# The last batches' output pairs of an attention and mixture-of-experts kernel, put in another order

## The chip, the cores and the metric

One NeuronCore of a Trainium2 chip runs the whole program. The metric is the device time of one execution in microseconds (us), lower is better.

## The reference

A transformer layer in float32, for an input x of 8 batches x 1024 tokens x 256 features:

```python
x = x + layernorm(attention(layernorm(x)))      # 16 heads of 16, causal mask
x = x + layernorm(ffn(layernorm(x)))

def ffn(hidden):                                # 8 experts, the best two of each token count
    scores = softmax(flat @ router_weight.T + router_bias)
    topk_w, topk_idx = top_k(scores, 2)
    gate, up = split(flat @ gate_up_proj[e] + gate_up_bias[e])
    act = (clip(up, -7, 7) + 1) * min(gate, 7) * sigmoid(1.702 * min(gate, 7))
    down = act @ down_proj[e] + down_bias[e]
    return sum over the two experts of topk_w * down
```

## The kernel before

The program has three stages with a barrier of all engines between them. **The attention stage** computes attention, the first residual sum, the router and the place of every token's row in a buffer `xs`, sorted by expert. **The expert stage** works through 136 tiles of 128 rows of `xs`, one expert each, and adds the results into `acc`. **The combine stage** normalises and adds the second residual. The change is in the attention stage only.

The attention stage is one list of **slots**, which every engine walks through in the same order; each engine's queue is in program order, and semaphores tie the queues together. There are 32 quads (four heads of one batch), and a quad takes `NE` = 12 slots: in slot g, TensorE makes four blocks of exponents' scores (line 853), ScalarE their exponentials (700), GpSimd masks the diagonal blocks (403, eight slots of twelve), TensorE weighs the values (872). Quad 31 ends with slot 383. Eighteen slots ahead runs the pass for the row maxima (TensorE 834, VectorE 485 and 488, in a ring of three PSUM banks), which ends at slot 365. A head of this pass takes three slots; in the trace, heads begin at 1194.6 us (slot 336), 1202.5 (339), 1227.9 (348) and 1237.0 (351). Attention's output goes to HBM twice a quad: the first half is stored at c = 6 of the quad (335), the second at c = 2 of the next (338), and with it the softmax denominators. c is the slot's number within its quad. At c = 0 SP also issues the twelve head loads of the quad after next (268, 270).

**Pairs.** The output side works on 32 pairs of token tiles (256 tokens), four to a batch; pair r has the start slot `C_AT[r]`. Relative to it:
- SP loads denominators and outputs at -8 (351, 355). VectorE inverts the denominators at -6 (580), SP stores them (317) and reloads them spread over partitions at -5 (324), with the pair's x behind (327), for which it first waits for the sum of pair r - 2 (`c_x1`).
- GpSimd multiplies outputs by inverses at -3 (431).
- TensorE projects at 0 and +1 (944), ScalarE copies at +1 (784), VectorE takes moments at +3 and +4 (600, 650), GpSimd turns them into a scale and a shift at +5 (438 to 444), ScalarE normalises at +6 (789), GpSimd adds x at +7 (452).
- The second norm runs likewise at +9, +10 and +11 (607, 650, 438 to 444, 798); SP stores the sum at +9 (358).
- TensorE transposes at +14 (965) and makes the router's logits at +15 and +16 (976); VectorE picks the best at +16 to +18 (655, 613, 619).

For the pairs before `LATE` = 28 the start slots are 12 apart: pairs 24 to 27 (batch 6) have 339, 351, 363 and 375. The last batch has 388, 391, 396 and 399.

**Groups.** The rows of a group of pairs are ranked together: `choose` on VectorE (520 to 533), `rank` on TensorE (988, 991), `place` on VectorE (545 to 567), which ends in the slot numbers `slot_i`. GpSimd then scatters the rows to `xs`, one indirect DMA of 128 rows for each tile and choice (462): 16 for a batch, 8 for half a batch. Batches 0 to 6 are a group each, the last batch is two. `G_AT` is the start of a group's last pair. A whole batch's scatters start 30 slots after it and are spread by `EVEN` over 36 slots; a half batch's start 22 after it, one a slot.

```python
    C_AT = [NE * (r + 4) + 3 for r in range(LATE)] + [NE * QUADS + d for d in (4, 7, 12, 15)]
    GROUPS = [range(PER * b, PER * b + PER) for b in range(B - 1)] + [range(LATE, LATE + 2), range(LATE + 2, PAIRS)]
    S_AT = [G_AT[n] + (EVEN[k] if n in STEADY else 22 + k) for n, k in SCATTERS]
```

Slots from 384 on have no attention work left: there only the pairs' own waits set the time, and each queue runs on in the order above. At the very end SP waits until all scatters have landed and writes one block of zeros behind each expert's rows (372 to 375, eight DMAs, each with an address read from SBUF first), and VectorE computes the table of tiles (659 to 685). SP waits for the zeros, and the barrier follows.

## Time and profile before

| what | us |
|---|---|
| median of three runs | 2316.2 (2313.4 to 2321.1) |
| the profiled execution | 2312.5 |
| its span, first to last instruction | 2310.7 |
| attention stage up to the last copy of its output | 1322.0 |
| from there to the expert stage's first load | 103.6 |
| from that load to the end of the span | 885.1 |

Busy time over the span, from the page of the profile: TensorE 2003.9 us (87%), VectorE 1687.1 (73%), ScalarE 1132.6 (49%), GpSimd 975.5 (42%). Such a share is a mean over stages with different limits, so it is to be read stage by stage. PE is TensorE's matmuls, PEld its weight loads, DVE VectorE, ACT ScalarE, POOL GpSimd, SP the queue that issues most DMAs (SPq). An arrow in a wait names what ended it.

### The profile page before, as it was taken

How to read it: one execution, taken by the hardware profiler on the slowest of the kernel's cores; microseconds unless marked ns; L12 is line 12 of the kernel's file. 1: busy time of each engine (PE TensorE's matmuls, PEld its weight loads, DVE VectorE, ACT ScalarE, POOL GpSimd, SP SyncE). 2: the span in 40 equal slices, each digit the busy share in tenths (PEclk: the TensorE clock that was granted, in tenths of full speed). 3: DMA queues.
4: the chain of work that ended last, by engine and by line, in shares of the span. 5: the costliest groups of instructions: out<-in, count | busy, mean ns of one | idle time of the engine just before them, and what ended most of it. 6: DMA issues, size and time to landing. Idle time of an engine off the chain costs nothing. (4 is left out here: it accounts for less than half of the span.)

```text
span 2310.7 us, 51852 instructions
## 1 busy us (share of the span) xinstructions
PE 2003.9 (87%) x13629; PEld 1307.3 (57%) x13630; DVE 1687.1 (73%) x5978; ACT 1132.6 (49%) x2647; POOL 975.5 (42%) x1583
## 2 busy tenths in 40 slices
PE   5499999999999999999989842999999999999960
PEld 4243444444444444444333331998898888888950
DVE  2487768787888888888868232777777777777768
ACT  3156667777777777777766720222222222222220
POOL 4122334445646465555544553333333333333326
PEclk9789999999999999999999955999999999999985
DMA  5926575767666666768584223887787778778766
GB/s 156 183 63 145 125 167 150 183 153 178 146 167 140 163 145 168 152 154 172 111 215 95 97 82 136 238 242 233 238 239 236 236 233 235 232 238 238 236 193 237
DMA packets 259627, 412.94 MB, mean 179 GB/s; under 512 B 37136, under 2 KB 194960, under 8 KB 253200
## 3 DMA queue, kind: packets, MB, share of 16 engines
q1 hardware_dynamic: 220432, 367.20, 58.6%
q0 software_dynamic: 29824, 35.54, 7.4%
q10 hardware_dynamic: 9216, 8.39, 1.1%
q8 instruction: 66, 1.08, 0.2%
q14 instruction: 89, 0.73, 0.1%
HBM read 288.30 MB, written 122.14 MB: 178 GB/s over the span
## 5 line engine op out<-in xcount | busy, mean ns | idle before, releaser
L700 ACT ACTIVATE pw<-ps_e 128x512 f32<-128x512 f32 (+3 forms) x1536 | 688.7, 493 | 310.2 <-PE ps_e L853 301.7
L1244 PE MATMUL ps_g<-x_t,w_gu 128*128 128x128 f32 x4384 | 541.7, 277 | 28.1 <-ACT x_t L1175 21.9
L834 PE MATMUL ps_s<-ks,qs 96*128 96x512 bf16 (+3 forms) x1536 | 492.9, 336 | 67.0 <-DVE mrow L499 34.1
L1244 PEld LDWEIGHTS ps_g<-x_t,w_gu 128*128 128x128 f32 x4384 | 515.2, 192 | 59.2 <-issue 49.1
L485 DVE CUSTOM_DVE_ANT_0 summed<-ps_s,c 128x128 bf16<-128x128 f32 (+3 forms) x1024 | 480.3, 482 | 83.2 <-PE ps_s L834 79.4
L853 PE MATMUL ps_e<-qs,ks 98*128 98x512 bf16 (+3 forms) x1536 | 487.1, 331 | 3.2 <-ACT pw L700 3.0
L488 DVE TENSOR_REDUCE cmax<-ps_s 128x1 f32<-128x512 f32 x512 | 351.5, 686 | 142.7 <-PE ps_s L834 139.9
L834 PEld LDWEIGHTS ps_s<-ks,qs 96*128 96x128 bf16 x1536 | 152.8, 101 | 405.0 <-issue 120.2
L872 PE MATMUL ps_o<-pw,vs 128*32 128x512 f32 (+3 forms) x3072 | 332.7, 506 | 4.9 <-ACT ot L714 2.8
L1196 ACT ACTIVATE d_y<-biased,weight 128x256 f32<-128x256 f32 x136 | 69.1, 508 | 490.3 <-DVE biased L1155 490.3
L403 POOL TENSOR_SCALAR_AFFINE_SELECT pw<-pw 128x512 f32<-128x512 f32 x256 | 162.1, 633 | 310.9 <-ACT pw L700 310.8
L1210 POOL DMA_INDIRECT acc<-d_y,place_now x136 | 214.8, 1580 | 120.5 <-issue 74.5
L1273 PE MATMUL ps_y<-space,act_h 128*128 x1088 | 258.1, 380 | 0.8 <-DVE act_h L1148 0.8
L1136 DVE TENSOR_SCALAR gate<-ps_g,space 128x128 f32<-128x128 f32 x548 | 154.4, 345 | 105.4 <-issue 94.1
L853 PEld LDWEIGHTS ps_e<-qs,ks 98*128 98x128 bf16 x1536 | 149.8, 98 | 110.2 <-ACT pw L700 19.9
L1273 PEld LDWEIGHTS ps_y<-space,act_h 128*128 128x128 f32 x1088 | 196.1, 190 | 22.6 <-issue 1.5
L1203 POOL TENSOR_TENSOR place_now<-place,c 128x1 int32<-128x1 int32 x136 | 24.9, 183 | 430.9 <-ACT d_y L1196 430.5
L1141 DVE TENSOR_SCALAR up<-ps_g,space 128x128 f32<-128x128 f32 x548 | 154.3, 344 | 9.0 <-PE ps_g L1244 0.2
L462 POOL DMA_INDIRECT xs<-c_h,slot_i x128 | 131.5, 1027 | 33.2 <-issue 32.6
L872 PEld LDWEIGHTS ps_o<-pw,vs 128*32 128x32 f32 x3072 | 60.9, 108 | 121.9 <-issue 80.1
L414 POOL DMA_DIRECT2D qs<-mrow x128 | 81.5, 637 | 109.6 <-DVE mrow L499 105.3
L1179 ACT ACTIVATE sig<-gate 128x512 f32<-128x512 f32 x137 | 86.3, 630 | 79.2 <-DVE gate L1136 79.2
(136 smaller groups left out, 2289.6 us busy)
## 6 DMA issues: line engine op xcount, KB each, us to landing
w_gu<-in_gate_up SPq DMA_DIRECT2D x138, 1024.0 KB, 5.0
qk_parts<-space SPq DMA_DIRECT2D x128, 192.0 KB, 7.2
qs<-qk_parts SPq DMA_DIRECT2D x192, 128.0 KB, 7.3
ks<-qk_parts SPq DMA_DIRECT2D x192, 128.0 KB, 7.8
d_xin<-xs SPq DMA_DIRECT2D x139, 130.5 KB, 2.5
v_aug<-space SPq DMA_DIRECT2D x32, 512.0 KB, 7.4
vs<-v_aug SPq DMA_DIRECT2D x32, 512.0 KB, 11.6
o_t<-ot SPq DMA_DIRECT2D x64, 256.0 KB, 2.8
```

The costliest lines, as they stand in the source:

```text
L403: pool.affine_select(diagonal, diagonal, [[0, 4], [1, P]], ALU.is_ge, 0.0, base=0, channel_multiplier=-1).then_inc(cut_done, 1)
L485: dve.tensor_tensor_reduce(summed[:, m % RJ, 0:w], ps_s[:, m % RS, 0:w], after[:, HALF - w:HALF], 1.0, LOWEST, ALU.add, ALU.max, dst).then ...
L488: dve.reduce_max(dst, ps_s[:, m % RS, 0:w], AX.X).then_inc(s_cmax, 1)
L700: act.activation(pw[:, n % RP, 0:w], ps_e[:, n % RE, 0:w], ACT.Exp, scale=SCALE).then_inc(e_done, 1)
L834: pe.matmul(ps_s[:, m % RS, 0:w], qs[0:ROWS, slot, i * P:(i + 1) * P], ks[0:ROWS, slot, k0:k0 + w], start=True, stop=True).then_inc(s_scor ...
L853: pe.matmul(ps_e[:, n % RE, 0:w], ks[0:ROWS_M, slot, j * P:(j + 1) * P], qs[0:ROWS_M, slot, q0:q0 + w], start=True, stop=True).then_inc(e_ ...
L872: last = pe.matmul(ps_o[s * QUAD:(s + 1) * QUAD, at:at + w], vs[:, u, j, s], pw[:, (g * 4 + s) % RP, 0:w], start=(j == 0), stop=(c + 1 in ...
L1136: last = dve.tensor_scalar(gate[:, u, m], ps_g[:, u, 0, m], b_gu[:, bass.ds(e, 1), m], LIMIT, ALU.add, ALU.min)
L1141: last = dve.tensor_scalar(up[:, m], ps_g[:, u, 1, m], b_gu[:, bass.ds(e, 1), KI + m], LIMIT + 1, ALU.add, ALU.min)
L1210: pool.indirect_dma_start(out=acc, out_offset=bass.IndirectOffsetOnAxis(place_now[:, u:u + 1], 0), in_=y[:, u], in_offset=None, compute_op ...
L1244: last = pe.matmul(ps_g[:, u, half, m % KI], w_gu[:, u, k, m * P:(m + 1) * P], x_t[:, u, k], start=(k == 0), stop=(k == KT - 1))
L1273: last = pe.matmul(ps_y[:, u, 0:D], act_h[:, u, m], w_dn[:, bass.ds(e, 1), m], start=(m == 0), stop=(m == KI - 1))
```

## The change

1. **Batch 6 every six slots.** `C_AT` of pairs 24 to 27 becomes 339, 345, 351 and 357.
2. **Halves.** Batch 6 is ranked in two groups of two pairs as well. The half groups get later steps relative to their start (`choose` 19 to 21, `rank` 23, `place` 23 to 26, scatters from 27 on). The scatters of batch 5 now follow one a slot from slot 357 on, those of batch 6 in slots 372 to 379 and 384 to 391, those of batch 7 in 415 to 422 and 433 to 440.
3. **The last pairs side by side.** `C_AT` of pairs 28 to 31 becomes 387, 388, 405 and 406. Loads and reciprocals of 30 and 31 stay as early as before by larger negative offsets (-17, -15, -12), while their projections come later in TensorE's order.
4. **VectorE multiplies and adds.** For pairs 24 to 31 the multiply by the inverses (offset -2 or -4) and the sum with x (+7) are VectorE's instead of GpSimd's. The reload of the inverses goes to offset -4 (pairs 24 to 29).
5. **Zero blocks on two queues.** Experts 0 to 3 by SP, 4 to 7 by ScalarE's queue, both after the same waits.

```diff
@@ -100,13 +100,16 @@
     A_AT = [BEGIN - 18 + 3 * a for a in range(EARLY)] + [BEGIN - 5, BEGIN + 2] + [NE * (a - 6) - 4 for a in range(6, PAIRS)]
     FIRST_EVEN = 6
     LATE = PAIRS - PER
-    C_AT = [NE * (r + 4) + 3 for r in range(LATE)] + [NE * QUADS + d for d in (4, 7, 12, 15)]
-    GROUPS = [range(PER * b, PER * b + PER) for b in range(B - 1)] + [range(LATE, LATE + 2), range(LATE + 2, PAIRS)]
+    C_AT = [NE * (r + 4) + 3 for r in range(LATE)] + [NE * QUADS + d for d in (3, 4, 21, 22)]
+    QUICK = LATE - PER
+    for r in range(QUICK, LATE):
+        C_AT[r] = C_AT[QUICK] + 6 * (r - QUICK)
+    GROUPS = [range(PER * b, PER * b + PER) for b in range(B - 2)] + [range(r, r + 2) for r in range(QUICK, PAIRS, 2)]
     G_AT = [C_AT[pairs[-1]] for pairs in GROUPS]
     SCATTERS = [(n, k) for n, pairs in enumerate(GROUPS) for k in range(len(pairs) * 2 * TOPK)]
-    STEADY = range(B - 1)
+    STEADY = range(B - 2)
     EVEN = [30 + d for turn in range(0, 4 * NE, NE) for d in (turn, turn + 6, turn + 7, turn + 9, turn + 10)]
-    S_AT = [G_AT[n] + (EVEN[k] if n in STEADY else 22 + k) for n, k in SCATTERS]
+    S_AT = [G_AT[n] + (30 + k if n == B - 3 else EVEN[k] if n in STEADY else 27 + k) for n, k in SCATTERS]
     SLOTS = range(A_AT[0] - 6, max(S_AT) + 2)
     MOMENTS = [(r, k) for slot, k, r in sorted((C_AT[r] + 3 + 6 * k, k, r) for r in range(PAIRS) for k in range(2))]
 
@@ -114,10 +117,15 @@
 
         return [n for n, start in enumerate(G_AT) if start + (steady if n in STEADY else late) == slot]
 
+    def rows_due(steady, quick, late, slot):
+
+        return [r for r, start in enumerate(C_AT) if start + (steady if r < QUICK else quick if r < LATE + 2 else late) == slot]
+
     def pairs_due(early, steady, slot):
 
         return [n for n, start in enumerate(A_AT) if start + (early if n < FIRST_EVEN else steady) == slot]
     LOADS = 12
+    NEVER = SLOTS.stop + NE * QUADS
     Q_STORES = 4
 
     base, table, expert_f = kept
@@ -255,6 +263,15 @@
 
             return sum(2 * PER * TOPK for e in range(b % 2, b, 2))
 
+        def clear_ends(engine, experts):
+
+            engine.wait_ge(zero_at_ready, 1)
+            for u in range(2):
+                engine.wait_ge(scattered[u], (T // P) * TOPK // 2 * 16)
+            for e in experts:
+                row = engine.value_load(zero_at[0:1, e:e + 1], min_val=0, max_val=E * REGION - P)
+                engine.dma_start(xs[bass.ds(row, P), :], blank[:, 0:ROW]).then_inc(zeros_out, 16)
+
         block = ctx.enter_context(nc.Block())
 
         @block.sync
@@ -311,11 +328,11 @@
                         load_heads(early)
                     for early in range(SETS):
                         load_values(early)
-                for r in due(C_AT, -6, g):
+                for r in rows_due(-6, -6, -15, g):
                     u, b, j = r % 2, r // PER, r % PER
                     sp.wait_ge(c_den, r + 1)
                     sp.dma_start(rden[r].rearrange("h (c t) -> (h c) t", c=P // H), den[:, u]).then_inc(rd_out[u], 16)
-                for r in due(C_AT, -5, g):
+                for r in rows_due(-5, -4, -12, g):
                     u = r % 2
                     sp.wait_ge(rd_out[u], (r // 2 + 1) * 16)
                     if r >= 2:
@@ -343,7 +360,7 @@
                 if 2 <= quad < 10 and c == 10:
                     sp.dma_start(acc_v[:, (quad - 2) * 2:(quad - 1) * 2],
                                  blank[:, 0:1024].unsqueeze(1).broadcast_to([P, 2, 1024])).then_inc(acc_zero, 16)
-                for r in due(C_AT, -8, g):
+                for r in rows_due(-8, -8, -17, g):
                     u, b, j = r % 2, r // PER, r % PER
                     sp.wait_ge(o_out[j // 2], (4 * b + 4) * 16)
                     if r >= 2:
@@ -367,12 +384,7 @@
                     sp.dma_start(b_dn.rearrange("p e d -> p (e d)"),
                                  down_bias.rearrange("(a e) d -> a (e d)", a=1).broadcast_to([P, E * D])).then_inc(biases_in, 16)
 
-            sp.wait_ge(zero_at_ready, 1)
-            for u in range(2):
-                sp.wait_ge(scattered[u], (T // P) * TOPK // 2 * 16)
-            for e in range(E):
-                row = sp.value_load(zero_at[0:1, e:e + 1], min_val=0, max_val=E * REGION - P)
-                sp.dma_start(xs[bass.ds(row, P), :], blank[:, 0:ROW]).then_inc(zeros_out, 16)
+            clear_ends(sp, range(0, E // 2))
             for u in range(2):
                 sp.wait_ge(x1_out[u], PAIRS // 2 * 16)
                 sp.wait_ge(o_out[u], QUADS * 16)
@@ -424,13 +436,13 @@
                     pool.wait_ge(a_negated, a + 1)
                     pool.wait_ge(a_rooted, a + 1)
                     pool.tensor_tensor(a_shift[:, u], a_minus[:, u], a_rstd[:, u], ALU.mult).then_inc(a_shifted, 1)
-                for r in due(C_AT, -3, g):
+                for r in due(C_AT[0:QUICK], -3, g):
                     u = r % 2
                     pool.wait_ge(o_loads[u], (r // 2 + 1) * KT * 16)
                     pool.wait_ge(rd_loads[u], (r // 2 + 1) * KT * 16)
                     pool.tensor_tensor(o_in[:, u], o_in[:, u], rd_in[:, u], ALU.mult).then_inc(c_on, 1)
-                for k, offset in enumerate((5, 10)):
-                    for r in due(C_AT, offset, g):
+                for k, offsets in enumerate(((5, 4, 4), (10, 10, 10))):
+                    for r in rows_due(*offsets, g):
                         u, n = r % 2, MOMENTS.index((r, k))
                         pool.wait_ge(c_agg, n + 1)
                         if r >= 2:
@@ -442,7 +454,7 @@
                         pool.wait_ge(c_negated, n + 1)
                         pool.wait_ge(c_rooted, n + 1)
                         pool.tensor_tensor(c_shift[:, k, u], c_minus[:, k, u], c_rstd[:, k, u], ALU.mult).then_inc(c_shifted, 1)
-                for r in due(C_AT, 7, g):
+                for r in due(C_AT[0:QUICK], 7, g):
                     u = r % 2
                     pool.wait_ge(c_yn, r + 1)
                     pool.wait_ge(cx_in[u], (r // 2 + 1) * 16)
@@ -574,16 +586,30 @@
                     if 0 <= m < HEADS * NM:
                         maximum(m)
                     if s == 0:
-                        for r in due(C_AT, -6, g):
+                        for r in rows_due(-6, -6, -15, g):
                             u = r % 2
                             dve.wait_ge(den_in[u], (r // 2 + 1) * 16)
                             dve.reciprocal(den[:, u], den[:, u]).then_inc(c_den, 1)
+                        for r in rows_due(NEVER, -2, -4, g):
+                            u = r % 2
+                            dve.wait_ge(o_loads[u], (r // 2 + 1) * KT * 16)
+                            dve.wait_ge(rd_loads[u], (r // 2 + 1) * KT * 16)
+                            dve.wait_ge(c_on, r)
+                            dve.tensor_tensor(o_in[:, u], o_in[:, u], rd_in[:, u], ALU.mult).then_inc(c_on, 1)
+                        for r in rows_due(NEVER, 7, 7, g):
+                            u = r % 2
+                            dve.wait_ge(c_yn, r + 1)
+                            dve.wait_ge(cx_in[u], (r // 2 + 1) * 16)
+                            dve.wait_ge(x1_out[u], r // 2 * 16)
+                            dve.wait_ge(c_hn, r - 1)
+                            dve.wait_ge(c_x1, r)
+                            dve.tensor_tensor(x1_sb[:, u], y[:, u], cx[:, u], ALU.add).then_inc(c_x1, 1)
                         for n in groups_due(19, 19, g):
                             choose(n, 0)
                     if s == 1:
-                        for n in groups_due(22, 19, g):
+                        for n in groups_due(22, 20, g):
                             choose(n, 1)
-                        for n in groups_due(27, 21, g):
+                        for n in groups_due(27, NEVER, g):
                             place(n, 0)
                         for a in pairs_due(-6, -16, g):
                             dve.wait_ge(ax_in[a % 2], (a // 2 + 1) * 16)
@@ -619,15 +645,17 @@
                                 last = dve.max_index(top_at[:, half, c], top[:, half, c], logits[:, half, c])
                             last.then_inc(c_ix, 1)
                     if s == 2:
-                        for n in groups_due(25, 19, g):
+                        for n in groups_due(25, 21, g):
                             choose(n, 2)
-                        for n in groups_due(27, 21, g):
+                        for n in groups_due(27, 24, g):
                             place(n, 1)
-                        for n in groups_due(28, 21, g):
+                        for n in groups_due(28, 25, g):
                             place(n, 2)
-                        for n in groups_due(29, 21, g):
+                        for n in groups_due(29, 26, g):
                             place(n, 3)
                     if s == 3:
+                        for n in groups_due(NEVER, 23, g):
+                            place(n, 0)
                         for a in due(A_AT, 2, g):
                             remainder(a, 0)
                         for a in due(A_AT, 4, g):
@@ -640,8 +668,8 @@
                             for t in range(2):
                                 last = dve.bn_aggr(a_mv[:, u, t], a_stats[:, t])
                             last.then_inc(a_agg, 1)
-                        for k, offset in enumerate((4, 9)):
-                            for r in due(C_AT, offset, g):
+                        for k, offsets in enumerate(((4, 3, 3), (9, 9, 9))):
+                            for r in rows_due(*offsets, g):
                                 u, n = r % 2, MOMENTS.index((r, k))
                                 dve.wait_ge(c_st, n + 1)
                                 if r >= 2:
@@ -811,6 +839,8 @@
                                 act.wait_ge(g_row, n)
                             act.activation(ex[:, 0:tiles], diff[:, 0:tiles], ACT.Exp).then_inc(g_ex, 1)
 
+            clear_ends(act, range(E // 2, E))
+
         @block.tensor
         def _(pe):
             used = []
@@ -1007,7 +1037,7 @@
                     if 0 <= g + 1 < NE * QUADS:
                         exp_scores(g + 1, s)
                     if s == 0:
-                        for n in groups_due(27, 20, g):
+                        for n in groups_due(27, NEVER, g):
                             rank(n)
                         for a in due(A_AT, 4, g):
                             q_or_k(a, 1, (1,))
@@ -1032,6 +1062,8 @@
                             turn_rows(r)
                         for r in due(C_AT, 16, g):
                             route(r, 1)
+                        for n in groups_due(NEVER, 23, g):
+                            rank(n)
                     if s == 2:
                         for a in due(A_AT, 3, g):
                             q_or_k(a, 1, (0,))
```

## Rows read from the trace of the kernel before

**Rows 1.** Busy time by stretch: us; busy (count) per engine; clock, DMA share, GB/s.
```profile
1178.90:1281.00 102.10, 89.46 (x599) 34.72 (x597) 77.80 (x302) 68.30 (x168) 46.41 (x81) 0.97 0.48 114
1281.00:1322.00 41.00, 35.01 (x253) 12.62 (x249) 6.09 (x35) 33.53 (x82) 23.67 (x37) 1.00 0.30 100
1322.00:1425.00 103.00, 28.47 (x111) 22.12 (x111) 24.80 (x132) 15.46 (x31) 56.13 (x81) 0.54 0.28 94
1425.00:2310.70 885.70, 773.93 (x5748) 720.63 (x5748) 693.16 (x2287) 205.84 (x429) 302.85 (x424) 0.95 0.77 233
```

**Rows 2.** Waits of the DMA queue SP, 1321 to 1425: total, times, longest.
```profile
SPq L372 <- DMA xs<-c_h,slot_i: 44.0, 1, 44.0
```

**Rows 3.** Timeline of GpSimd (POOL): start, us, instruction, idle before it.
```profile
1338.22 1.26 POOL L431 TENSOR_TENSOR o_in<-o_in,rd_in 128x512 f32<-128x512 f32 x1 [6.02 <-DMA rd_in<-rden]
...
1371.89 1.04 POOL L462 DMA_INDIRECT xs<-c_h,slot_i  x1 [0.49 <-issue]
...
1410.66 0.96 POOL L462 DMA_INDIRECT xs<-c_h,slot_i  x1 [0.30 <-issue]
```

**Rows 4.** Timeline of VectorE (DVE).
```profile
1346.59 0.35 DVE L580 RECIPROCAL den<-den 128x32 f32<-128x32 f32 x1 [13.54 <-DMA den<-o_t]
...
1378.47 0.17 DVE L655 TENSOR_TENSOR logits<-ps_w,bias_r 128x16 f32<-128x16 f32 x1 [2.65 <-PE ps_w L976]
...
1381.70 0.16 DVE L567 CAST slot_i<-slot_f 128x8 int32<-128x8 f32 x1
...
1389.74 0.42 DVE L685 TENSOR_SCALAR table<-entry 128x140 int32<-128x140 f32 x1
```

**Rows 5.** Timeline of the DMA queue SP.
```profile
1325.19 0.47 SPq L338 DMA_DIRECT2D o_t<-ot  x1
1329.19 0.56 SPq L351 DMA_DIRECT2D den<-o_t  x1
...
1331.99 0.33 SPq L317 DMA_DIRECT2D rden<-den  x1
1334.62 1.21 SPq L324 DMA_DIRECT2D rd_in<-rden  x2
...
1414.35 8.46 SPq L375 DMA_DIRECT2D xs<-blank  x8
1425.64 0.37 SPq L1091 DMA_DIRECT2D d_xin<-xs  x1
```

**Rows 6.** Timeline of ScalarE (ACT): the last copy of attention's output.
```profile
1321.40 0.60 ACT L714 ACTIVATE ot<-ps_o 128x512 f32<-128x512 f32 x1 [2.31 <-PE ps_o L872]
```

**Rows 7.** Groups by shape, 1322 to 1425: xcount | busy us, mean ns.
```profile
L462 POOL DMA_INDIRECT xs<-c_h,slot_i x37 | 36.7, 991 | 11.9 <-issue 11.9
L944 PE MATMUL ps_s<-w_o,o_in 128*128 128x256 f32 x32 | 14.4, 622 | 19.7 <-POOL o_in L431 19.7
...
L976 PE MATMUL ps_w<-w_r,h_t 128*128 128x8 f32 x40 | 8.9, 349 | 6.6 <-ACT h_t L806 6.6
...
L441 POOL TENSOR_TENSOR c_rstd<-c_var,c 128x2 f32<-128x2 f32 x9 | 6.3, 704 | 0.0
L798 ACT ACTIVATE c_h<-x_sb,c_shift,c_rstd 128x256 f32<-128x256 f32 x10 | 5.5, 593 | 5.6 <-POOL c_shift L444 5.6
L452 POOL TENSOR_TENSOR x_sb<-c_y,c_x 128x512 f32<-128x512 f32 x4 | 5.1, 1266 | 0.1
...
L965 PE MATMUL ps_e<-c,c_h 128*128 128x128 f32 x16 | 4.4, 429 | 0.4 <-ACT c_h L798 0.4
...
L607 DVE BATCH_NORM_STATS2 c_stats<-x_sb 128x6 f32<-128x256 f32 x8 | 3.0, 416 | 7.6 <-POOL x_sb L452 7.6
```

**Rows 8.** Two lines of VectorE over the whole span: ns min/median/max.
```profile
L1148 DVE TENSOR_TENSOR act_h<-mid,sig x137: 691/691/745, 1439.2 to 2234.1; 128x512 f32<-128x512 f32 x137
...
L567 DVE CAST slot_i<-slot_f x9: 164/170/614, 507.7 to 1381.7; 128x16 int32<-128x16 f32 x7, 128x8 int32<-128x8 f32 x2
```

**Rows 9.** VectorE's wait at pair 24; head loads at 1224.5 to 1231, us to landing.
```profile
1186.26 0.35 DVE L580 RECIPROCAL den<-den 128x32 f32<-128x32 f32 x1 [6.90 <-DMA den<-o_t]
...
ks<-qk_parts SPq DMA_DIRECT2D x6, 128.0 KB, 8.0
```

## The prediction

> **What bounds the kernel now.** First the busy time of each engine by stage [rows 1]: TensorE is busy 87% up to 1322 us and again from 1425 us on, and between them it does 28 us of work in 103. So the kernel is bound by TensorE's pace in two long stages and by a hole of some 103 us between them, where the last batches are finished, routed and scattered and the experts cannot start. The change touches only the hole and the 140 us before it. What ends the hole is told by the DMA queue's waits [rows 2]: SP waits 44.0 us, once, for the scatters of rows to have landed. GpSimd's timeline shows why [rows 3]: from 1371.89 to 1411.62 it issues nothing but scatters, 31 of them without a break, 1.27 to 1.29 us apart. VectorE had the last slot numbers at 1381.86 [rows 4]; the 30 us after that are backlog, because the first scatters of batch 6 stood in GpSimd's queue behind its own multiply for pair 30, which waited 6.02 us for a load [rows 3], and behind the norms of batch 7. SP then issues the eight zero blocks in 8.46 us [rows 5], and the experts' first load goes out at 1425.64.
>
> Why the slot numbers come so late is in SP's timeline [rows 5] and VectorE's [rows 4]: the last pair's denominators are asked for only after SP has worked through pair 30's reload (1334.62) and then waited for pair 28's sum, and VectorE stands 13.54 us for them.
>
> **Part 1, the tail replayed.** I put the new order of each queue beside the measured durations. The reference point is the end of the last copy of attention's output, 1322.0 [rows 6], held fixed here. Pairs 28 and 29 are loaded before it on SP (slots 379 to 384 instead of 380 to 386), so that TensorE projects them without a gap: sixteen products of 0.62 us, less overlap, take 7.2 us as two groups of eight took 3.6 each [rows 7], until 1329.2. Then for each pair comes the chain [rows 7]: copy 0.6 (as [rows 6]), two moments calls 0.8 and aggregates 0.3, GpSimd's power and its three small partners 1.35 (0.70 and three of 0.2, overlapped), ScalarE's two calls 1.1, the sum, moments and aggregates 1.1, GpSimd 1.35, ScalarE 1.1, four transposes 1.1, copy 0.6, eight routing products 1.9. The sum on VectorE goes at 0.69 instead of 1.27 on GpSimd, by the nearest VectorE row of that size with two inputs [rows 8]. One pair alone would need 12 us; two abreast share GpSimd, ScalarE and TensorE, and the second ends about 17 us after its projection, at 1346.
>
> Meanwhile SP stores the last output block at 1322.1, three microseconds earlier than now (1325.19 [rows 5]), and goes on with the steps as they took: 4.0 us to the denominators' load, 2.4 to the reciprocal, then 2.6 until the reload may go, 1.2 to issue and 2.4 to land [rows 3 to 5]. The multiplies of pairs 30 and 31 can run on VectorE at about 1338 and 1339; they are queued there behind the second moments of pair 29 (1338), so they hold nothing up. TensorE takes their projections only after it has routed pair 29, at 1346, and ends them at 1353.6. Their chain is again some 17.5 us, with the eight small calls that rank the first half threaded into it: logits at 1371.2, against 1378.47 now [rows 4]. From the logits to the slot numbers it is 3.4 us as now: 1374.6, **7.3 us earlier**.
>
> GpSimd in the tail: batch 6's second eight scatters go out from about 1320 (7 x 1.27 us, done before pair 28's moments are ready at 1330; the eighth stands between the two norms, at no cost since pair 29's moments come 1 us later). The first half of batch 7 has slot numbers at 1360.2; its eight scatters run until 1373.9. So when the last eight come due at 1374.6 GpSimd is free, and they end at 1384.8. Backlog behind the last slot numbers falls from 29.8 to 10.2 us: **19.6 us**. VectorE's table of tiles takes 8 us from its last slot numbers [rows 4] and is ready at 1383; it stays hidden.
>
> **Part 2, zero blocks.** Four on SP and four on ScalarE's queue: 8.46 us of issue become 4.2, **4.2 us** off. Bounds: nothing, if the two queues' issues hinder each other, and 5 if ScalarE issues at the 0.4 us of a plain DMA; nearest is SP's own row.
>
> Tail together: 7.3 + 19.6 + 4.2 = 31.1 us off. Bounds of the replay: I may have missed up to 8 us of waits between engines, or reckoned 4 too much.
>
> **Part 3, what batch 6 now costs before 1322.** The multiply and the sum of four pairs move to VectorE: 8 x 0.69 = 5.5 us. Pair 26 wholly and half of pair 27 move from behind slot 366 to before it: some 3 us of VectorE, at most 5 of TensorE (a pair's projection, transposes and routing take 3.6 + 1.1 + 1.9 in the tail, at its slower clock), 5 of ScalarE. In this stretch VectorE has 24.3 us free of 102.1, of which 6.9 are one wait [rows 1, 9], and TensorE 12.6. But where the exponents are narrow (slots with c of 9 to 2) VectorE feeds TensorE with hardly a gap, and four of the eight moved calls and two added moments passes fall there: about 5.5 us lost. Then two new waits. Pair 25's and pair 27's denominators are loaded at slots 337 and 349, directly behind the twelve head loads of slots 336 and 348, of which each lands 8.0 us after its issue [rows 9]. VectorE would ask for them at slots 339 and 351, 6 to 8 us after the load is issued: 1 to 3 us of waiting each, say 4 together. Queued behind the reciprocal are the row maxima, and for them TensorE waits. Behind slot 366, where ScalarE sets the pace (33.5 of 41 us [rows 1]), about 2.5 us of its work are gone. Sum: 5.5 + 4 - 2.5 = **7 us later**; bounds 0 (all in gaps) and 15 (each load waits as long as the one row of such a wait, 6.90 us [rows 9]).
>
> GpSimd gets 24 scatters into slots 357 to 379 (30 us) and loses four multiplies and four sums (10 us); it was busy 23.7 of the last 41 us with seven scatters in them, so some 29 now. Cost nothing; if the cover is gone, the diagonal masks come late and TensorE waits up to 0.6 us a slot.
>
> A rule speaks against part 3. Once, a VectorE cast took 614 ns where its median is 170 [rows 8]; it ran beside a 0.7 us mask on GpSimd. Of nine such casts one was held, so the meeting is rare. The Trainium skill (SBUF — State Buffer, Who interferes with whom) says that a VectorE instruction with two SBUF inputs and a GpSimd instruction that reads SBUF take turns on a shared port pair, the later one standing still. By that rule each of the eight moved calls could wait out a mask, some 0.6 us each, and the sum would end 5 us later than mine, at 2297; by the rows here the calls keep 0.69. The held cast fits that rule's picture; no row shows a two-input call held.
>
> The expert and combine stages (886 us [rows 1]) see the same rows, tiles and order: no change.
>
> **The sum.** -31.1 + 7 = -24. The profiled execution took 2312.5 us (span 2310.7): 2288.4. The median of the runs is 3.7 us above that execution, so I give **2292 us**.
>
> **Rivals.**
> A. The scatters stay the bound. GpSimd cannot place 24 scatters beside masks and row stores before 1322, and half of batch 6's sixteen slide into the tail in front of pair 28's norms. For: it is GpSimd that ends the tail now. Against: its 29 us of work in 41. Price: up to 8 x 1.27 = 10 us, with the waits of part 3 at their upper end another 6: gain 8, 2308 us. Chance 0.13.
> B. Slower: VectorE's in-order waits before 1322. Moved to VectorE, each multiply waits for the reload, and each reciprocal for its load, in front of the row maxima that TensorE needs; on GpSimd such a wait was free. Price: a wait like the one at 1179 to 1186 costs its 6.9 us. It decides once these waits sum to 31 us, that is when eight waits (two for each of pairs 24 to 27) average 3.9 us. All eight at 6.9 would give 2316 - 31 + 55 = 2340 us. For: the loads of slots 337 and 349 do stand behind head loads. Against: the other reloads are issued two slots (5.8 us) ahead, with 2.4 to land, in stretches where the DMA is half idle (share 0.48 [rows 1]). Chance 0.07.
> C. The change does not shorten the chain, since pair 31's projection, now at 1354, is still there at 1350 to 1354: the batch-6 scatters vanish from the end but the side-by-side pairs get in each other's way, eating the 7.3 us and a further 10. With part 3 at 10 that leaves 4 us: 2312, no difference that can be told. Chance 0.07.
> D. Part 3 is free and the replay exact: -31 to -34, 2283 us. Chance 0.12.
> Forecast as above: 0.61.
>
> A measurement of this kernel tells about 0.3%, 7 us, from no change. Forecast, D and A are faster by more (0.86), C is the same (0.07), B slower (0.07). The range: from D with 3 us spare, 2280, to A, 2309; outside it are C, B and the edge of A, under 0.2.
>
> **What would show it.** Right: in the waits of SP the scatters' wait falls from 44 us to some 10 or 15; GpSimd's last unbroken run holds eight scatters instead of 31; the last slot numbers come some 7 us after today's minus part 3's shift, that is near 1381 again with the last output copy near 1329; SP and ScalarE issue four zero blocks each, within 4.3 us; the first expert load is at about 1401. VectorE shows waits of 1 to 3 us at the reciprocals of pairs 25 and 27. Wrong: an output copy later than 1337 (B), more than ten scatters in one run at the end (A), logits of pair 31 over 60 us after the output copy (C), or a copy before 1324 (D).

## The result, and the profile after

| | before | after |
|---|---|---|
| median of 4 runs each, same chip, us | 2314.8 (2310.1 to 2321.1) | 2286.1 (2280.4 to 2291.9) |
| span of the profiled execution | 2310.7 | 2278.6 |
| up to the 13th-last store of attention's output (`o_t`) | 1119.6 | 1111.8 |
| b: from there to the end of its last copy | 202.4 | 211.2 |
| c: from that to the experts' first load | 103.6 | 80.9 |
| d: from that load to the end (expert stage, combine) | 885.1 (817.7, 67.3) | 874.8 (807.1, 67.7) |

The ratio is 0.9874, 95% interval [0.9833, 0.9916]: 1.3% faster, 28.7 us between the medians. The first stretch, which the change doesn't touch, took 1110.9 to 1120.6 us in the fourteen profiled executions of this study without regard to the kernel, so its 7.8 us here are chance; a single b or c scatters by some 3 us either way.

Busy time by stretch of the kernel after: the 41 us before the last output copy, the tail, and the experts [rows 1]; columns as there.

```profile
1282.00:1323.00 41.00, 33.99 (x259) 11.17 (x251) 7.52 (x52) 31.55 (x79) 24.96 (x35) 1.00 0.27 94
1323.00:1403.80 80.80, 25.62 (x90) 20.38 (x90) 28.41 (x117) 14.30 (x27) 33.69 (x55) 0.56 0.31 101
1403.80:2278.60 874.80, 774.76 (x5748) 723.55 (x5748) 689.54 (x2286) 205.44 (x429) 301.23 (x424) 0.95 0.78 236
```

The tail lost 23 us, and GpSimd's busy time in it fell from 56 to 34 us. The last line is the one nobody forecast: the same 5748 products as before take 10 us less wall time, with TensorE's busy time the same.

SP's waits after, 1321 to 1404 us [rows 2]:

```profile
SPq L270 <- DMA xs<-c_h,slot_i: 28.2, 1, 28.2
SPq L375 <- DVE x_sb L606: 20.5, 2, 19.6
SPq L392 <- DMA xs<-blank: 2.9, 1, 2.9
```

GpSimd's timeline after [rows 3]: the last scatter of batch 6's second half but one, and the idle time until pair 28's norms; the idle time until pair 30's; the last scatter of the first half of batch 7; and the only run left behind the last slot numbers.

```profile
1329.34 0.96 POOL L474 DMA_INDIRECT xs<-c_h,slot_i  x1 [0.30 <-issue]
1335.83 0.20 POOL L450 TENSOR_TENSOR c_var<-c_mv,c 128x2 f32<-128x2 f32 x1 [5.54 <-DVE c_mv L678]
...
1361.32 0.20 POOL L450 TENSOR_TENSOR c_var<-c_mv,c 128x2 f32<-128x2 f32 x1 [13.52 <-DVE c_mv L678]
...
1379.60 0.96 POOL L474 DMA_INDIRECT xs<-c_h,slot_i  x1 [0.31 <-issue]
1382.29 1.43 POOL L474 DMA_INDIRECT xs<-c_h,slot_i  x1 [1.73 <-DVE slot_i L579]
...
1391.86 0.96 POOL L474 DMA_INDIRECT xs<-c_h,slot_i  x1 [0.30 <-issue]
```

VectorE's timeline after [rows 4]: the multiplies and the reciprocals of the last pairs, then the last logits and slot numbers.

```profile
1324.97 0.69 DVE L598 TENSOR_TENSOR o_in<-o_in,rd_in 128x512 f32<-128x512 f32 x1 [4.94 <-issue]
1329.52 0.69 DVE L598 TENSOR_TENSOR o_in<-o_in,rd_in 128x512 f32<-128x512 f32 x1 [3.85 <-DMA rd_in<-rden]
1333.09 0.35 DVE L592 RECIPROCAL den<-den 128x32 f32<-128x32 f32 x1 [2.87 <-DMA den<-o_t]
...
1338.48 0.35 DVE L592 RECIPROCAL den<-den 128x32 f32<-128x32 f32 x1 [2.73 <-DMA den<-o_t]
...
1347.05 0.69 DVE L598 TENSOR_TENSOR o_in<-o_in,rd_in 128x512 f32<-128x512 f32 x1 [0.94 <-DMA rd_in<-rden]
...
1377.93 0.17 DVE L683 TENSOR_TENSOR logits<-ps_w,bias_r 128x16 f32<-128x16 f32 x1 [2.17 <-PE ps_w L1006]
...
1381.85 0.17 DVE L579 CAST slot_i<-slot_f 128x8 int32<-128x8 f32 x1
```

The timelines of the queue SP [rows 5] and of ScalarE [rows 6] after:

```profile
1309.29 0.32 SPq L352 DMA_DIRECT2D o_t<-ot  x1
1314.05 0.56 SPq L368 DMA_DIRECT2D den<-o_t  x1
...
1317.80 2.04 SPq L334 DMA_DIRECT2D rden<-den  x2
1320.66 1.22 SPq L341 DMA_DIRECT2D rd_in<-rden  x2
...
1395.45 4.11 SPq L273 DMA_DIRECT2D xs<-blank  x4
1403.84 0.37 SPq L1123 DMA_DIRECT2D d_xin<-xs  x1
```

```profile
1322.37 0.60 ACT L742 ACTIVATE ot<-ps_o 128x512 f32<-128x512 f32 x1 [1.64 <-PE ps_o L902]
...
1395.40 4.14 ACTq L273 DMA_DIRECT2D xs<-blank  x4
```

From the last copy (ends at 1322.97) the slot numbers take 59.1 us, against 59.9 before; the backlog of scatters is 10.8, against 29.8. In this execution the whole gain of the tail is thus backlog and zero blocks, and the 7.3 us that the replay had found for the chain aren't there.

### The profile page after: what moved, and what is told of

Read it like the earlier page. It is cut to its first block and busy times, and to the rows that moved or that the text cites. A ratio compares the mean times of both kernels' runs of the same rounds, so it can differ in the third digit from the quotient of the medians.

```text
span 2278.6 us, 51879 instructions
## 1 busy us (share of the span) xinstructions
PE 1999.7 (88%) x13630; PEld 1310.2 (57%) x13631; DVE 1695.6 (74%) x6010; ACT 1132.6 (50%) x2648; POOL 958.4 (42%) x1567
## 5 line engine op out<-in xcount | busy, mean ns | idle before, releaser
L1242 POOL DMA_INDIRECT acc<-d_y,place_now x136 | 212.8, 1565 | 96.6 <-issue 77.1
```

Of the source, the lines that this page charges most:

```text
L1242: pool.indirect_dma_start(out=acc, out_offset=bass.IndirectOffsetOnAxis(place_now[:, u:u + 1], 0), in_=y[:, u], in_offset=None, compute_op ...
```

## The experiments

Each was timed in rounds with the kernel before, on the same chip. Stretches b, c and d are those of the table above; a ratio is to the kernel before.

**How far both kernels repeat.** No edit.

> The kernel of before, unchanged, to see how far stages that nobody edits vary. The profile is cut at four marks: (a) start to the store of the first half of quad 27's predecessor block at 1119.6 us in before, 1111.8 in after; (b) from there to the end of the last output copy: 202.4 and 211.2; (c) from that to the first load of the experts: 103.6 and 80.9; (d) the rest: 885.1 and 874.8. Theory M (only b and c belong to the change, +8.8 and -22.8; a and d vary from execution to execution): b and c come within 3 us of before's, a and d anywhere, a from 1110 to 1122, d from 874 to 887. Theory R (a and d are also shorter because of the change): a within 2 us of 1120 and d at least 883.

> The changed kernel, unchanged. Theory M: b 211 and c 81, each within 3 us, a and d anywhere in the ranges named for the kernel of before; ratio to before near 1 - 14/2315 = 0.994 when a and d even out. Theory R: a within 2 us of 1112, d within 2 us of 875, ratio 0.986 to 0.988.

Measured: before again 2309.1 us, ratio 1.0016 [0.9994, 1.0037], with b 199.6, c 103.8, experts 821.0. After again 2279.8, ratio 0.9867 [0.9842, 0.9893], with b 208.1, c 77.5, experts 807.3. The slot numbers came 56.1 us behind the copy here, so 1 to 4 us of the chain's 7.3 are there. The first stretch, 1112.3 and 1117.6 us, did vary as theory M has it, but the expert stage shows its 12 to 14 us again: that isn't chance, and for it theory M falls.

**Zero blocks on one queue again.**

```diff
-            clear_ends(sp, range(0, E // 2))
+            clear_ends(sp, range(0, E))
...
-            clear_ends(act, range(E // 2, E))
```

> After, with all eight zero blocks on SP again. Theory 1 (issue bounds the zero blocks; two queues halve it, but the landing takes 1.5 us longer): c grows by 2.8 us to 83.7, the eight issues take 8.5 us instead of 4.1. Theory 2 (the writes themselves are the bound): c unchanged within 1 us.

Measured: 2283.2 us, ratio 0.9904 [0.9872, 0.9935]. SP's timeline of this kernel:

```profile
1391.24 8.46 SPq L273 DMA_DIRECT2D xs<-blank  x8
1402.61 0.37 SPq L1122 DMA_DIRECT2D d_xin<-xs  x1
```

The first load goes 11.4 us after the first block's issue, against 8.4 in the kernel after (1395.45 to 1403.84): two queues gain 3.0 us, not 4.2. The issue halves, from 8.46 to 4.1, but the load follows the last issue 4.3 us later instead of 2.9. c itself was 79.5, where 83.7 was expected, since the slot numbers came 54.6 us behind the copy here. Nothing in front of them differs from the kernel after, so this is a third reading of its chain: 59.1, 56.1 and 54.6 us, against 59.4 to 61.1 in the six kernels with the old order.

**Zero blocks on two queues, alone,** in the kernel before.

```diff
-            for e in range(E):
...
+            clear_ends(sp, range(0, E // 2))
...
+            clear_ends(act, range(E // 2, E))
```

> Before, with part 5 alone: zero blocks on SP and ScalarE's queue. By the run with one queue taken out of after: the issue takes 4.1 us instead of 8.2 to 8.5, and 1.1 us of it are lost again to a longer landing, so c is 3 us below before's 103.7 (100.7), and the time 3 us (0.1%) shorter. The expert stage (817.7 and 821.0 us in the two profiles of before, 806.5 to 809.4 in the four of after and its variants): if ScalarE's or SP's part of the change shortens it, it is near 808 here; if not, 817 to 821. I expect the latter.

Measured: 2295.8 us, ratio 0.9926 [0.9894, 0.9958]; c 101.0, b 200.4, experts 816.7. The stretch gives the 3 us again. The medians differ by 13; some 3 more can be the expert stage's, and what the rest is stays open, since the profiled execution (span 2299.0 against 2304.2 and 2310.7) does not lay it to any stage.

**The last four pairs one after another again,** on their old slots (30 and 31 one later); all else as changed.

```diff
-    C_AT = [...] + [NE * QUADS + d for d in (3, 4, 21, 22)]
+    C_AT = [...] + [NE * QUADS + d for d in (4, 7, 13, 16)]
...
-                for r in rows_due(-8, -8, -17, g):
+                for r in rows_due(-8, -8, -8, g):
...
```

> After, with the last four pairs one after another again (start slots 388, 391, 397, 400, loads relative to each pair as for the others), multiplied and summed on VectorE. From the last output copy to the last slot numbers it was 59.9 us in before and 59.1 in after, where 52.6 were forecast. Theory 1 (side by side gains what it was meant to, and a later load took it back): in turn it is 65 us or more, c 87 or more. Theory 2 (what shortened the tail is the early scatters alone, and side by side is worth nothing): 57 to 62 us, c 79 to 84.

Measured: 2279.3 us, ratio 0.988 [0.9851, 0.9908]; c 78.1. GpSimd's timeline of this kernel, its last run of sixteen:

```profile
1371.54 1.04 POOL L474 DMA_INDIRECT xs<-c_h,slot_i  x1 [8.11 <-DVE slot_i L579]
...
1391.53 0.96 POOL L474 DMA_INDIRECT xs<-c_h,slot_i  x1 [0.30 <-issue]
```

The last slot numbers come at 49.1 us behind the copy, which neither theory allowed for, earlier than side by side (54.6 to 59.1), but so close behind those of the first half that 18.4 us of scatters follow. The two cancel: side by side as placed here is worth nothing. In this order TensorE also projects pair 31 (1348.80 to 1352.55) in front of pair 28's transposes (1352.34) and not behind them, which the last two experiments take up.

**Multiplies and sums of the eight pairs on GpSimd again.**

```diff
-                for r in due(C_AT[0:QUICK], -3, g):
+                for r in rows_due(-3, -2, -4, g):
...
-                for r in due(C_AT[0:QUICK], 7, g):
+                for r in due(C_AT, 7, g):
...
```

VectorE's two blocks of calls for these pairs are taken out.

> After, with part 4 undone: the multiplies and sums of pairs 24 to 31 on GpSimd again. Theory 1 (VectorE's extra calls cost before the last output copy, and free GpSimd behind it): b falls by 3 us from 207 to 211, c grows by 5 us or more from 77.5 to 80.9, as each multiply waits for its reload in front of scatters and norms. Theory 2 (they cost and bring nothing): b and c as in after within 3 us. Expert stage: VectorE's program is 40 instructions shorter than in after and still 19 longer than in before, GpSimd's as long as in before. If it stays near 808, GpSimd's program is not what shortens it.

Measured: 2287.9 us, ratio 0.9898 [0.9865, 0.993]; b 211.3, c 77.0, experts 815.6. Neither the 5.5 us that the calls on VectorE were to cost before the copy nor the gain of 0.6 us a sum in the tail is there: b and c stay where they were. What makes this kernel slower than the changed one is its expert stage, 8 us longer; this is the edit that takes VectorE's program back towards its old length.

**Nothing but longer programs.** In the compiled programs the change puts the start of each engine's expert loop further down: by 59 instructions on VectorE, 29 on ScalarE, 3 on TensorE. These are counts from the compiled programs and stand in no trace. These three kernels are the kernel before with waits added that are long satisfied, at the end of the attention stage, on TensorE alone (+3 instructions), on VectorE alone (+59), and on all three.

```diff
+            for _ in range(117):
+                dve.wait_ge(s_scores, 1)
...
+            for _ in range(57):
+                act.wait_ge(e_scores, 1)
...
+            for _ in range(5):
+                pe.wait_ge(e_scores, 1)
```

> Before, with waits on a semaphore that is long set at the end of TensorE's attention program, so many that the expert loop begins at the same place of TensorE's program as in after (three instructions later). Theory P (the expert stage is 11 us shorter because of the place of TensorE's loop in its program): expert stage 806 to 810. Theory V (the place of VectorE's loop) or theory O (what happens in the chip before it, such as the order of DMAs): 817 to 821.

> Before, with such waits at the end of VectorE's attention program, behind the table of tiles, so that its expert loop begins 59 instructions later, as in after. Theory V: expert stage 806 to 810 and the whole 11 us shorter than before (2296 against 2307), though nothing is computed otherwise. Theories P and O: 817 to 821.

> Before, with waits on semaphores long set at the end of TensorE's, VectorE's and ScalarE's attention programs, so that their expert loops begin at the same places as in after (3, 59 and 29 instructions later); GpSimd's and SP's cannot be moved forward. So far the expert stage took 817.7, 821.0 and 820.4 us with VectorE's loop at its old place and nothing on ScalarE, 816.7 and 815.6 with ScalarE's and SP's moved, 812.1 with VectorE's moved alone, 806.5 to 809.4 with all. Theory L (the place of the loops in their programs is all there is to it): 807 to 811, and VectorE's waits in front of the gate that nothing in the profile explains fall from 88 to 60 us or less. Theory O (something else of the change shortens it, for instance the order in which rows reached memory): 812 or more.

| | this / before, us | ratio | b | c | experts |
|---|---|---|---|---|---|
| TensorE | 2313.5 / 2309.0 | 1.0015 [0.9988, 1.0041] | 205.1 | 103.8 | 820.4 |
| VectorE | 2305.7 / 2309.0 | 0.9985 [0.9965, 1.0004] | 202.6 | 105.3 | 812.1 |
| all three | 2300.5 / 2312.4 | 0.9951 [0.9927, 0.9974] | 201.7 | 104.2 | 807.9 |

A kernel with added waits and nothing else is 0.5% faster, and its expert stage takes the 808 us of the changed kernel. VectorE alone is in between: a stage of 812, where its theory said 806 to 810, and a time that can't be told from the kernel before's. How that looks is told by VectorE's largest group of the stage, 1450 to 2180 us (xcount | busy, mean ns | idle before, and what ended it), of the kernel before, with the long VectorE program, with all three, and of the kernel after:

```profile
L1136 DVE TENSOR_SCALAR gate<-ps_g,space 128x128 f32<-128x128 f32 x500 | 140.8, 345 | 94.2 <-issue 87.6 <-PE ps_g L1244 6.6
```

```profile
L1138 DVE TENSOR_SCALAR gate<-ps_g,space 128x128 f32<-128x128 f32 x504 | 141.9, 344 | 89.8 <-issue 46.3 <-PE ps_g L1246 43.5
```

```profile
L1143 DVE TENSOR_SCALAR gate<-ps_g,space 128x128 f32<-128x128 f32 x505 | 142.3, 345 | 88.9 <-issue 60.2 <-PE ps_g L1251 28.7
```

```profile
L1168 DVE TENSOR_SCALAR gate<-ps_g,space 128x128 f32<-128x128 f32 x504 | 141.9, 344 | 87.8 <-issue 58.9 <-PE ps_g L1276 28.9
```

These calls are as long as ever, and four to five more of them fit into the same 730 us. The idle time in front of them falls less than it seems: the part that ends with "issue", with nothing in the profile waited for, goes from 87.6 to 46 to 60 us, but most of what it loses is now put down to TensorE, and the whole goes from 94.2 to 88 to 90. TensorE, which sets the pace here (774 us busy of 818), shows the gain itself, in its products for gate and up; the kernel before, with all three, and the kernel after:

```profile
L1244 PE MATMUL ps_g<-x_t,w_gu 128*128 128x128 f32 x4010 | 494.2, 276 | 24.1 <-ACT x_t L1175 21.9 <-DMA w_gu<-in_gate_up 2.2
```

```profile
L1251 PE MATMUL ps_g<-x_t,w_gu 128*128 128x128 f32 x4065 | 500.6, 276 | 13.7 <-ACT x_t L1182 9.7 <-DMA w_gu<-in_gate_up 2.5 <-issue 0.9
```

```profile
L1276 PE MATMUL ps_g<-x_t,w_gu 128*128 128x128 f32 x4067 | 501.4, 276 | 12.7 <-ACT x_t L1207 10.4 <-issue 1.8
```

Its idle time falls by 10 to 11 us, nearly all of it waits for ScalarE's copy of the transposed rows, `x_t`; with the long VectorE program alone it is 17.6. That a longer program in front of the loops does it is shown; that it is the loops' place in it, and by what mechanism, isn't. It is not program code loaded anew for each tile: from 1430 to 2180 us the DMA queues carry five packets of instructions in the kernel before, three with all three engines' waits and one in the kernel after.

**Twelve slots a pair for batch 6, as before,** but ranked in halves and multiplied on VectorE.

```diff
-        C_AT[r] = C_AT[QUICK] + 6 * (r - QUICK)
+        C_AT[r] = C_AT[QUICK] + 12 * (r - QUICK)
```

> After, with batch 6 every twelve slots again (start slots 339, 351, 363, 375), still ranked in halves; its second eight scatters then stand in slots 402 to 409, after the last output copy. b was 199.6 to 205.1 us in before and its padded forms, 207.1 to 211.3 in after and its variants; c was 103.6 to 105.3 and 77.0 to 80.9. Theory 1 (the six-slot spacing is what costs 7 us before the copy, and GpSimd has room for eight scatters in the tail, where it stood 5.5 and 13.5 us idle in after): b 200 to 204, c 77 to 82, the kernel some 6 us faster than after. Theory 2 (the eight scatters are missed in the tail): c 87 to 91, no faster than after.

Measured: 2278.4 us, ratio 0.9856 [0.9819, 0.9894]; b 208.9, c 76.0, backlog 10.8, experts 806.9. The second half of batch 6 now scatters inside the tail and still costs nothing. GpSimd's timeline of this kernel:

```profile
1339.34 1.04 POOL L474 DMA_INDIRECT xs<-c_h,slot_i  x1 [0.49 <-DVE slot_i L579]
...
1347.01 0.96 POOL L474 DMA_INDIRECT xs<-c_h,slot_i  x1 [0.30 <-issue]
```

b is not the 200 to 204 us of theory 1, but it hides two things. Here it is cut at the stores of attention's output, which stand in slots 342, 362 and 378 (means of the profiled executions, us):

| | kernels | to 342 | 342 to 362 | 362 to 378 | 378 to the last copy |
|---|---|---|---|---|---|
| old order | 6 | 90.0 | 57.7 | 39.8 | 14.4 |
| changed, six slots a pair | 6 | 92.7 | 62.8 | 39.9 | 13.9 |
| changed, twelve slots a pair | 2 | 91.7 | 58.3 | 46.2 | 14.6 |

Between slots 342 and 362 the close spacing costs 5.1 us, and with twelve slots all but 0.6 of it is gone. The two twelve-slot kernels (this one and the last of the study) lose it again behind slot 362, where TensorE's granted clock was 0.89 and 0.82 in the mean, against 0.96 to 1.00 in the twelve others. In this kernel TensorE was busy 5.4 of the 8 us at whose end the clock fell to its lower level, 1.2 GHz; columns as in [rows 1]:

```profile
1280.00:1288.00 8.00, 5.41 (x38) 1.40 (x36) 3.19 (x11) 4.91 (x15) 5.88 (x7) 0.96 0.45 134
1288.00:1296.00 8.00, 7.47 (x37) 1.70 (x36) 0.00 (x0) 5.30 (x14) 6.77 (x12) 0.50 0.29 103
```

In them TensorE waited 0.47 and 1.16 us for masks of GpSimd, which had batch 5's scatters between them. So the close spacing does cost some 4.5 us, and the tail doesn't need it. Both profiled executions with twelve slots show the lower clock there; whether the spacing brings it isn't shown.

**The last two pairs projected ahead of the transposes of the two before.** The kernel after, where TensorE stands idle 11.68 us and then has pair 31's projection behind pairs 28's and 29's transposes and routing:

```profile
1330.27 5.49 PE L974 MATMUL ps_s<-w_o,o_in 128*128 128x256 f32 x12 [2.41 <-issue]
1347.43 1.09 PE L995 MATMUL ps_e<-c,c_h 128*128 128x128 f32 x4 [11.68 <-ACT c_h L826]
...
1352.35 1.87 PE L1006 MATMUL ps_w<-w_r,h_t 128*128 128x8 f32 x8 [0.75 <-ACT h_t L834]
1354.07 6.55 PE L974 MATMUL ps_s<-w_o,o_in 128*128 128x256 f32 x16
```

```diff
-    C_AT = [...] + [NE * QUADS + d for d in (3, 4, 21, 22)]
+    C_AT = [...] + [NE * QUADS + d for d in (3, 4, 15, 16)]
...
-                for r in rows_due(-6, -6, -15, g):
+                for r in rows_due(-6, -6, -9, g):
...
-                        for r in rows_due(NEVER, -2, -4, g):
+                        for r in rows_due(NEVER, -2, 2, g):
```

> After, with the projections of pairs 30 and 31 ahead of the transposes of 28 and 29 in TensorE's order (start slots 399 and 400, loads at the same slots as in after). In after TensorE stands 11.7 us idle before those transposes and begins pair 30 only 8 us after its multiply was done. Theory 1 (this order is what ate the forecast 7.3 us of the tail): the last slot numbers come 49 to 53 us after the last copy instead of 56 to 59, c 70 to 75. Theory 2 (the chains of two rounds share GpSimd, ScalarE and VectorE anyway, or the first half's scatters come later for it and run into the last): c 76 to 81.

Measured: 2274.9 us, ratio 0.9835 [0.981, 0.9859]; c 71.3. TensorE's timeline of this kernel:

```profile
1325.13 5.04 PE L974 MATMUL ps_s<-w_o,o_in 128*128 128x256 f32 x12 [2.26 <-DVE o_in L598]
1341.00 2.04 PE L974 MATMUL ps_s<-w_o,o_in 128*128 128x256 f32 x4 [10.82 <-DVE o_in L598]
1343.32 4.47 PE L974 MATMUL ps_s<-w_o,o_in 128*128 128x256 f32 x12 [0.27 <-DVE o_in L598]
1347.63 1.04 PE L995 MATMUL ps_e<-c,c_h 128*128 128x128 f32 x8
```

The projections end at 1347.8 instead of 1360.6 (its last copy is 2.8 us earlier), the slot numbers come 48.6 us behind the copy instead of 55 to 59, the backlog is 11.8. The kernel with the last four pairs one after another had them at 49.1, in the same order of projections and transposes. This is the fastest kernel of the study: it beats the kernel before clearly and the changed one by 0.3%, at the edge of what can be told: the two intervals overlap.

**Both of the last two edits together.**

> The changed kernel with both edits that lowered its time one at a time: the last two pairs' loads, multiplies and projections ahead of the transposes of the pairs before them, and batch 6 back at twelve slots a pair. Theory 1 (the tail's length is set by when the last pair's projection gets its operand, and the six-slot spacing buys nothing because eight scatters more fit into the tail): the stretch from the last output copy to the experts' first load is 69 to 73 us against 71.3 with the one edit, the backlog behind the last slot numbers 10 to 12, the kernel 2270 to 2277 us, no slower than either edit alone. Rival (the six-slot spacing is needed once the tail is shorter: the twelve-slot kernel's eight extra scatters now come in front of pair 28's and 29's small GpSimd calls or behind the last slot numbers): the backlog is over 15 us or the last slot numbers later than 52 us after the copy, and the kernel 2278 us or more. In both the expert stage takes 806 to 809 us, since the engines' programs are as long as the changed kernel's.

Measured: 2277.7 us, ratio 0.986 [0.9833, 0.9886]; b 212.8, c 71.0, slot numbers at 49.3, backlog 11.0, experts 807.6. The tail is as short as with the first edit alone and no shorter, so it needs no six-slot spacing. The median is 0.7 us over what was expected and no better than either edit's; b, the longest of all, has the stretch at the lower clock in it.

## Why the prediction was right, and where its steps were not

The forecast of 2292 us was 6 above the 2286.1 measured, inside 2280 to 2309, and its kind, faster, held. Against the sum of −24 us stand −28.7, but that is nearer than the terms deserve. Means over the profiled executions: b of the six kernels with the old order in it (before, again, zeros alone, three padded) is 202.0, of the six with the change's six slots a pair 209.3.

- **Backlog, −19.6 forecast.** 29.8 to 10.8, **−19.0**. Right, with its mechanism: eight scatters behind the last slot numbers, the others in GpSimd's idle time. It carries the gain.
- **Slot numbers 7.3 us earlier.** Measured 0.8, 3.8 and 5.3, in the three kernels with this chain. The step that failed is the start of the replay, "TensorE projects them without a gap ... until 1329.2". They ended at 1335.8. Pair 28's denominators could be asked for only at 1314.05, 4.8 us after the issue of the output store in front of them (1309.29), where it was 2.0 in the kernel before (1307.58 to 1309.57); SP works through both pairs' loads, then their inverses, then their reloads, so pair 28's reload went out at 1320.66 and pair 29's multiply ran at 1329.52, 5.2 us after its own reload's issue ended (1324.37), not 2.4. The replay counted eight and eight products, but not the operands' way. From the projections' end it was good: pair 31's logits 17.3 us behind its projection (1360.6 to 1377.93), 17.5 forecast. The replay saw that the multiplies "hold nothing up" and left out the reciprocals: that of pair 31 waits 2.73 us in front of pair 29's moments (1338.48), and TensorE stands idle 11.68 us until the transposes of pairs 28 and 29, with pairs 30 and 31 queued behind them, though their operands were ready at 1347.7. Projecting these first took 6 to 10.5 us off, which shows that this place was the limit; that order stood in the replay ("only after it has routed pair 29"), its price did not.
- **Zero blocks, −4.2.** The mechanism is right and the size too large: **−3.0**, since the blocks land later behind the shorter issue.
- **Part 3, +7.** b is 209.3 against 202.0, **+7.3**. The total is right; by the table above 2.7 us of it lie before slot 342, 5.1 from 342 to 362, and nearly none behind, where 2.5 were to come back. The two waits came as forecast, in VectorE's timeline after

```profile
1179.05 0.35 DVE L592 RECIPROCAL den<-den 128x32 f32<-128x32 f32 x1 [7.51 <-DMA den<-o_t]
...
1200.36 0.35 DVE L592 RECIPROCAL den<-den 128x32 f32<-128x32 f32 x1 [3.24 <-DMA den<-o_t]
...
1238.31 0.35 DVE L592 RECIPROCAL den<-den 128x32 f32<-128x32 f32 x1 [0.98 <-DMA den<-o_t]
```

  (3.24 and 0.98 us at pairs 25 and 27; the first line is pair 24's, as in [rows 9]). The 5.5 us put on moved calls and two moments passes aren't the calls': with the calls back on GpSimd the two stretches 342 to 350 and 354 to 362 were 1.2 us shorter together and b no shorter. Of the 5.1 us, 4.5 go with the spacing, that is with the work of pairs 26 and 27 moved forward, which the forecast had put into gaps but for two moments passes. What the 2.7 before slot 342 are beyond pair 25's wait stays open.
- **Expert and combine stages, "no change".** This step was wrong, and it is the largest error: −12.5 us (817.7, 821.0 and 820.4 to 807.1 and 807.3). The step looked at what the stage computes. It didn't ask how long the engines' programs in front of its loops are, and the padded kernels show that longer ones alone give it.
- **The sum.** Backlog −19.0, slot numbers −3.3 (mean of three), zero blocks −3.0, part 3 +7.3, experts −12.5: −30.5, against −28.7 between the medians. The steps as forecast, with the tail at what it measured (−25.3) and no expert term, would have given −18, some 2298: inside the range too. That 2292 came so near was luck: the tail was reckoned 6 us too good and the expert stage's 12.5 left out.
- **The signs named.** The last run holds eight scatters, four zero blocks stand on each queue within 4.2 us, the first load is at 1403.8 (1401 forecast), the waits of 1 to 3 us are there. Wrong were the scatters' wait of SP, 28.2 where 10 to 15 was said, which only tells that SP came to it earlier, at 1367 us, and the output copy at 1323.0 instead of 1329: that is the first stretch's 7.8 us of chance, and by the sign as written would have spoken for rival D.
- **Rivals.** A fell: GpSimd had seven of the eight scatters of batch 6's second half done at 1330.3, before pair 28's norms at 1335.83, and the eighth between two norms, as forecast. B fell: VectorE's waits for denominators in front of the row maxima sum to 11.7 us, and none for reloads stands before slot 366; that is 4.8 more than before, where 31 were needed. C named the right place (pair 31's projection, which ended at 1360.6) and the wrong size. D's total, 2283, was nearest of all but by the experts' term, which it didn't have.
- **The port rule.** The prediction counted one held cast of nine; it was two, both of 0.61 us beside a mask of 0.70 us (1107.87 and 1255.96). Of the 112 moved calls in the seven kernels that have them on VectorE 109 took 0.66 to 0.69 us. One took 0.98, begun 0.22 us after a mask on GpSimd. VectorE's and GpSimd's timelines of the last kernel above:

```profile
1323.76 0.98 DVE L598 TENSOR_TENSOR o_in<-o_in,rd_in 128x512 f32<-128x512 f32 x1 [0.80 <-issue]
```

```profile
1323.54 0.65 POOL L415 TENSOR_SCALAR_AFFINE_SELECT pw<-pw 128x512 f32<-128x512 f32 x1
```

  That is what the Trainium skill (SBUF — State Buffer, Who interferes with whom) describes, the later of the two held, so a row now shows a two-input call held, by 0.3 us. As a price it stays small: the two others outside took 0.75 and 0.76, so the 5 us for eight held calls, by which the sum would have been 2297, are not there, and the rows' 0.69 was the right figure. More often GpSimd was the later one: a small call of it that takes 0.20 us alone took 0.62, begun 0.13 us after a sum on VectorE. VectorE's and GpSimd's timelines after:

```profile
1339.68 0.69 DVE L606 TENSOR_TENSOR x_sb<-c_y,c_x 128x512 f32<-128x512 f32 x1
```

```profile
1339.81 0.62 POOL L450 TENSOR_TENSOR c_var<-c_mv,c 128x2 f32<-128x2 f32 x1 [1.08 <-DVE c_mv L678]
```

## What to carry to other kernels

When the last engine's backlog ends a stage, cut the work into smaller groups early enough that it drains before the last result, and leave the engine queue free in front of the operand that the last chain starts from: in-order engines pay for a finished small step (a reciprocal, a transpose) standing in front of the one that is late. Replay the tail from the landing of the first operand, not from the free engine. Before a shorter stretch is laid to an edit, look at the granted clock in its parts. And before a loop stage's gain is put down to an edit elsewhere, pad the kernel before to the same program length: here that alone was worth 0.5%.

## What the runs showed of the hardware

- The length of the engines' programs in front of a loop changes its pace. 59 instructions more on VectorE took the expert stage from 820 to 812 us, 29 more on ScalarE and 3 on TensorE with them to 808, while 3 on TensorE alone did nothing (820.4). The mean times of gate's calls and of gate and up's products are equal to 1 ns; TensorE's idle time in front of these products fell from 24 to 14 us in 730.
- Splitting eight small DMAs over two issuing queues halved the issue (8.46 to 4.1 us) and brought the load that waits for them forward by 3.0 us only.
- A two-input call on VectorE and a GpSimd call that overlap can hold the later one: a multiply took 0.98 instead of 0.69 us, and a GpSimd call 0.62 instead of 0.20.
- TensorE's granted clock fell to 1.2 GHz near the end of the attention stage, though the engine had work: it was busy 5.4 of the 8 us at whose end the clock fell, and 7.5 of the next 8, at 0.50.
